# A fused attention and quantised feed-forward kernel: the feed-forward stage written out in full, with three pairs of PSUM banks for gate and up, and with its steps reordered

## The chip, the cores and the metric

The kernel runs on one core of one Trainium2 chip. The metric is the device time of one execution in microseconds (us); the median of three runs of the kernel before is 2051.89 us (2051.29 to 2052.78). A measurement of this kernel tells a difference of about 0.2%, some 4 us, from none.

## What is computed

```python
x = x + xattn(layernorm(x), ctx_2048, Wq, Wk, Wv, Wo)     # 16 x 256 tokens of 512, 16 heads of 128
x = x + ffn(layernorm(x), w_gate, w_up, w_down)

def ffn(x):                                   # w_gate, w_up: 2048 x 512; w_down: 512 x 2048
    gate = q_act(x) @ q_w(w_gate).T
    up   = q_act(x) @ q_w(w_up).T
    inter = silu(gate) * up
    return q_act(inter) @ q_w(w_down).T
# q_act, q_w: block quantisation along the last axis in blocks of 32: a shared power of two from the
# block's largest magnitude, each element rounded to a few bits, clipped (at 7.5 or 6.0), scaled back
```

## The kernel before, in words

The program is written by hand for each of the five queues (TensorE, VectorE, ScalarE, GpSimd and the SyncE queue that issues most DMAs), with semaphores between them. Each queue works strictly in the order written.

**The attention stage** comes first and takes the first 1690 us or so. The change leaves it as it is. At its end every queue goes over into the feed-forward stage.

**The feed-forward stage.** The 4096 tokens are 32 tiles of 128 rows (`TILES`). The 2048 intermediate columns of a tile are four quarters of 512, counted `u = 4 t + k`; two quarters are a pair, `v = 2 t + h`, and there are 64 pairs (`PAIRS`). For a pair the work goes round all engines:

- TensorE: `gate_up` makes one quarter, four matmuls into a gate bank and four into an up bank (line 1097). It may start when the bank pair is free, that is, when VectorE has done `inner` of the quarter two before. For the first quarter of a tile it also waits for the tile's transposed rows (`xqT_loaded`, two buffers).
- ScalarE: `silu` of the gate bank into SBUF (line 688).
- VectorE: `inner` multiplies this with the up bank (line 831). When both quarters of a pair are there, `reduce` takes the magnitudes of the blocks (line 1008), `scales` makes the power (line 876) and its inverse (line 882), and `round_a` rounds one half to fp8 (line 1019).
- GpSimd: `round_b` rounds the other half (line 557).
- VectorE: `clip` of the whole pair to bf16 (line 1028). In the order of VectorE it stands in the next pair, between its two `inner`.
- ScalarE: `scale` copies the powers to bf16 (line 734). GpSimd: `rescale` multiplies the clipped pair with them (line 566); in GpSimd's order `rescale(v-1)` stands ahead of `round_b(v)`.
- SyncE: `transpose_inner` (line 373) transposes the pair by DMA into one of four slots. Behind that of an even pair `2 t` it issues `load_x_tile(t + 2)` (line 356), the transposing DMA of the rows of the tile two further on from a DRAM scratch. Both go by the one queue, in order.
- TensorE: `down` multiplies the pair with the down weights, eight matmuls into one of two banks (line 1220), three pairs behind the gate and up products.
- ScalarE: `move_down` copies the finished sum of a tile to SBUF (line 728). GpSimd: `add_out` adds it to the output in DRAM by an accumulating DMA (line 571).

The last half of the last pair goes another way: TensorE transposes it against an identity matrix (line 1266), and ScalarE and VectorE copy it out. The last two tiles are added to the attention rows, which are still in SBUF, by VectorE (lines 1081, 1085), and stored by plain DMAs (line 393).

The last attention batch is normalised and quantised within the feed-forward stage: `LAST_STEPS` gives after which pair VectorE does a step of it (lines 837 to 871), `POOL_STEPS` after which pair GpSimd does one (lines 480 to 499). So VectorE and GpSimd are written out for the first 18 tiles (`STRAIGHT`) and loop over the rest; TensorE and ScalarE loop from tile 4, SyncE from tile 2.

Of the kernel before, what the change touches and what calls it, by code (L numbers as in the profile page):

```python
# [36 lines left out]
ALU = mybir.AluOpType  # L37
# [21 lines left out]
STRAIGHT = 18  # L59
# [22 lines left out]
def build(nc, kvt, wattn, wffn, xtok, out):  # L82
# [4 lines left out]
    with ctx:  # L87
# [25 lines left out]
        identb = sb("identb", P, BF16)  # L113
# [34 lines left out]
        def free_part(chunk, part, pc, pieces):  # L148
# [5 lines left out]
        iqT = free_part(2, 1, 4, 4).bitcast(BF16)  # L154
        sil = free_part(0, 0, 0, 2).bitcast(F32)
# [5 lines left out]
        i_scale = sb("inner_scale", 32, BF16)[:, :]  # L161
# [8 lines left out]
        pLast = [bS[:, 0:256].bitcast(BF16), bC[:, 0:256].bitcast(BF16)]  # L170
        last_rows = [acc[:, 0:D], acc[:, D:2 * D]]
        gate = [bPT, bQK]
        up = [bX, bV]
# [16 lines left out]
            iqT_loaded0 iqT_loaded1 iqT_loaded2 iqT_loaded3 down_done d_moved out_stored0 out_stored1 last_q last_tr last_moved last_added last_stored0 last_stored1"""  # L190
        sm = {n: sem(n) for n in names.split()}
        sm["first_loaded"] = [sem(f"first_loaded{pc}") for pc in range(PIECES)]
# [71 lines left out]
        def _(eng):  # L264
# [103 lines left out]
            def transpose_inner(v, at):  # L368

                wait_apart(eng, "i_q", v + 1)  # L370
                if not isinstance(v, int) or v >= 4:
                    wait_apart(eng, "down_done", v - 3)
                eng.dma_start_transpose(half(iqT, at, 1024).rearrange("p (j f) -> p j f", j=8),
                                        half(iq, at % 2, 1024)).then_inc(sm[f"iqT_loaded{at}"], 16)

            def tile(t, at, more=True, last=False):
                transpose_inner(2 * t, 2 * at)
                if more:
                    load_x_tile(t + 2, at)
                if not last:  # L380
                    transpose_inner(2 * t + 1, 2 * at + 1)
# [6 lines left out]
            tile(TILES - 2, 0, more=False)  # L388
            tile(TILES - 1, 1, more=False, last=True)
            eng.wait_ge(sm["x1_stored"], 16 * B)  # L390
            for j in range(2):
                eng.wait_ge(sm["last_added"], j + 1)
                eng.dma_start(out[TILES - 2 + j], last_rows[j]).then_inc(sm[f"last_stored{j}"], 16)
            for at in range(2):
                eng.wait_ge(sm[f"out_stored{at}"], 8 * TILES - 16)
            for j in range(2):
                eng.wait_ge(sm[f"last_stored{j}"], 16)
# [3 lines left out]
        def _(eng):  # L401
            eng.memset(ident[:, :], 0.0).then_inc(sm["ident_ready"], 1)
            eng.memset(identb[:, :], 0.0).then_inc(sm["ident_ready"], 1)
            eng.memset(powers[:, 0:1], -0.5).then_inc(sm["ident_ready"], 1)
            eng.memset(powers[:, 1:2], 1e-5).then_inc(sm["ident_ready"], 1)
            eng.wait_ge(sm["ident_ready"], 4)
            for m in (ident, identb):
                eng.affine_select(out=m[:, :], in_=m[:, :], compare_op=ALU.not_equal, fill=1.0, base=0,
                                  pattern=[[-1, P]], channel_multiplier=1).then_inc(sm["ident_ready"], 1)
# [151 lines left out]
            def rescale(v, h):  # L561

                wait_apart(eng, "i_clip", v + 1)
                wait_apart(eng, "i_scale_done", v + 1)
                q = half(iq, h, 1024)
                eng.tensor_tensor(by_block(q), by_block(q), spread(i_scale), ALU.mult).then_inc(sm["i_q"], 1)  # L566
# [7 lines left out]
            def tile(t, at, out_=True, last_batch=False):  # L574
                for h in range(2):
                    v = 2 * t + h
# [3 lines left out]
                    if last_batch and v == 0:  # L580
                        store_x1(B - 1, acc[:, 0:2 * D].rearrange("p (t d) -> p t d", t=2))
                    step = POOL_STEPS.get(v) if last_batch else None
                    if step == "rstd":
                        tile_rstd(B - 1)
                    for j in range(2):
                        if step == f"round{j}":
                            x_round(TILES - 2 + j, j)
                        if step == f"rescale{j}":
                            x_rescale(TILES - 2 + j)
                if out_:  # L590
                    add_out(t - 2, at)

            tile(0, 0, out_=False, last_batch=True)
            tile(1, 1, out_=False, last_batch=True)
            eng.wait_ge(sm["x1_stored"], 16 * B)
            for t in range(2, STRAIGHT):
                tile(t, t % 2, last_batch=True)
            with eng.Fori(STRAIGHT // 2, TILES // 2) as m:
                for a in range(2):
                    tile(2 * m + a, a)  # L600
# [3 lines left out]
            eng.tensor_tensor(by_block(q), by_block(q), spread(i_scale[:, 0:NBLK]), ALU.mult).then_inc(sm["i_q"], 1)  # L604

        @block.scalar
        def _(eng):
# [75 lines left out]
            def silu(t, k):  # L683
                u = 4 * t + k
                eng.wait_ge(sm["gu_done"], u + 1)
                if not isinstance(t, int) or u >= 2:
                    eng.wait_ge(sm["inner_done"], u - 1)
                eng.activation(half(sil, k % 2), gate[k % 2][:, :], ACT.Silu).then_inc(sm["silu_done"], 1)
# [41 lines left out]
            def scale(v):  # L730
                eng.wait_ge(sm["i_pow_done"], v + 1)
                if not isinstance(v, int) or v > 0:
                    eng.wait_ge(sm["i_q"], v)
                eng.activation(i_scale, i_pow, ACT.Copy, scale=16.0).then_inc(sm["i_scale_done"], 1)

            def tile(t, at, begun=0, out_=True):
                for h in range(2):
                    for k in (2 * h, 2 * h + 1):
                        if k >= begun:
                            silu(t, k)  # L740
                    if out_ and h == 0:
                        move_down(t - 2, at)
                    scale(2 * t + h)

            tile(0, 0, begun=2, out_=False)
            tile(1, 1, out_=False)
            tile(2, 0)
            tile(3, 1)
            with eng.Fori(2, TILES // 2) as m:
                for a in range(2):  # L750
                    tile(2 * m + a, a)
            eng.wait_ge(sm["last_tr"], 1)
            eng.activation(half(iqT, 6), pLast[0], ACT.Copy).then_inc(sm["last_moved"], 1)
# [3 lines left out]
        def _(eng):  # L757
            eng.wait_ge(sm["ident_ready"], 6)
# [67 lines left out]
            def inner(t, k):  # L826
# [4 lines left out]
                eng.tensor_tensor(half(inter, k), up[k % 2][:, :], half(sil, k % 2), ALU.mult  # L831
# [190 lines left out]
            def clip(t, at, h):  # L1022
                v = 2 * t + h
                eng.wait_ge(sm["i_round_a"], v + 1)
                wait_apart(eng, "i_round_b", v + 1)
                if not isinstance(t, int) or t >= 1:
                    wait_apart(eng, f"iqT_loaded{2 * (1 - at) + h}", 8 * (t - 1 - (1 - at)) + 16)
                eng.tensor_scalar(half(iq, h, 1024), half(i8, h, 1024), 7.5 / 64, -7.5 / 64, ALU.min, ALU.max  # L1028
                                  ).then_inc(sm["i_clip"], 1)
# [17 lines left out]
            def tile(t, at, begun=0, last_batch=False):  # L1047
                for h in range(2):
                    v = 2 * t + h
                    if 2 * h >= begun:  # L1050
                        inner(t, 2 * h)
                    if h == 1:
                        clip(t, at, 0)
                    elif not (isinstance(t, int) and t == 0):
                        clip(t - 1, 1 - at, 1)
                    if 2 * h >= begun:
                        inner(t, 2 * h + 1)
                    reduce(v, h)
                    scales(v)
                    round_a(v, h)  # L1060
                    if last_batch and v == 0:
                        add_rows(B - 1, 0)
                        add_rows(B - 1, 1)
                    if last_batch and v in LAST_STEPS:
                        last_step(*LAST_STEPS[v])

            tile(0, 0, begun=2, last_batch=True)
            for t in range(1, STRAIGHT):
                tile(t, t % 2, last_batch=True)
            with eng.Fori(STRAIGHT // 2, TILES // 2) as m:  # L1070
                for a in range(2):
                    tile(2 * m + a, a)
# [232 lines left out]
```

## Time and profile before

| what | value |
|---|---|
| median of the runs | 2051.89 us |
| the profiled execution | 2051.55 us |
| its span in the profile | 2050.0 us, so 1.55 us lie around it |
| granted TensorE clock, mean | 0.999 of full speed |
| instructions | 45754 |
| DMA traffic | 193.26 MB, mean 94 GB/s |

Times in the profile count from the span's start. PE is TensorE's matmuls, PEld its weight loads, DVE is VectorE, ACT is ScalarE, POOL is GpSimd, SPq the queue of SyncE. All buffers of the feed-forward stage lie in the space of the attention weights, so the profile names them all attn_weights; which one it is follows from the line. A row of the timeline has the start, the duration, the engine, the line, the operation, what it writes and reads, and in brackets how long the engine was idle before it and what released it. Matmul ends are modelled, so the time of a group of matmuls is best read from the start of one group to the start of the next.

### The profile page before, as it was taken

To read this page: it belongs to the slowest core of one execution; us is meant where nothing else is said; L and a number is where in the kernel's file an instruction comes from. 1 tells how busy PE (TensorE), PEld (TensorE's weight loads), DVE (VectorE), ACT (ScalarE), POOL (GpSimd) and SP (SyncE) were. 2 spreads that over 40 slices of the span, in tenths; PEclk is the share of its full clock that TensorE was granted. 3 is DMA by queue.
4 is the path that set the end of the run, shared out by engine and by line. 5 is a ranking of instruction groups with operands and counts; after the bars stand their busy time and mean duration, and the time that the engine had idled before them with its cause. 6 is when DMAs were issued, how large, how long until landed. Compare 5 with 4: busy or idle time off the path is not lost. (4 is left out here: it accounts for less than half of the span.)

```text
span 2050.0 us, 45754 instructions
## 1 busy us (share of the span) xinstructions
PE 2021.3 (99%) x15430; PEld 1506.2 (73%) x15430; DVE 1536.7 (75%) x3340; ACT 1000.2 (49%) x2682; POOL 740.2 (36%) x881
## 2 busy tenths in 40 slices
PE   8999999999999999999999999999999999999998
PEld 6888878788888888878888888888888874444443
DVE  6767777777777877777777777776665558888887
ACT  8955545455555455555454555455555453222332
POOL 5422232323333333323333333331111006777776
PEclk9999999999999999999999999999999999999999
DMA  8834444444444444444444445443333274454554
GB/s 257 211 72 84 86 91 86 91 90 86 90 91 91 91 88 87 91 91 91 91 86 87 90 89 91 91 86 72 69 70 71 55 168 80 78 92 83 88 87 85
DMA packets 455038, 193.26 MB, mean 94 GB/s; under 512 B 418400, under 2 KB 431200, under 8 KB 454848
## 3 DMA queue, kind: packets, MB, share of 16 engines
q1 hardware_dynamic: 432640, 139.52, 35.3%
q0 software_dynamic: 15872, 44.97, 9.2%
q10 hardware_dynamic: 6336, 6.29, 1.0%
q8 instruction: 112, 1.84, 0.4%
q14 instruction: 78, 0.64, 0.1%
HBM read 61.21 MB, written 27.26 MB: 43 GB/s over the span
## 5 line engine op out<-in xcount | busy, mean ns | idle before, releaser
L1097 PE MATMUL b_qk<-kvT,attn_weights 128*128 128x256 f16 x3072 | 377.2, 273 | 3.5 <-DVE qk L762 2.9
L1097 PE MATMUL b_v<-attn_weights,kvT 128*128 128x256 f16 x3072 | 377.2, 273 | 0.0
L1097 PE MATMUL b_qk<-xT,attn_weights 128*128 128x256 f16 x3072 | 377.2, 273 | 0.0
L654 ACT ACTIVATE prob<-b_s,nmax 128x256 f32<-128x256 f32 x514 | 239.2, 470 | 276.1 <-DVE nmax L923 274.2
L1097 PEld LDWEIGHTS b_qk<-kvT,attn_weights 128*128 128x128 f16 x3072 | 300.2, 98 | 92.7 <-issue 4.9
L950 DVE SCALAR_TENSOR_TENSOR psplit<-prob,rrec,psplit 128x256 f16<-128x256 f32 x514 | 306.5, 637 | 79.2 <-ACT psplit L664 79.2
L762 DVE SCALAR_TENSOR_TENSOR qk<-b_qk,qk 128x512 f16<-128x512 f32 x256 | 176.7, 690 | 246.0 <-ACT qk L610 238.4
L610 ACT ACTIVATE qk<-b_qk 128x512 f16<-128x512 f32 x256 | 152.5, 596 | 426.4 <-PE b_qk L1097 426.2
L1097 PEld LDWEIGHTS b_qk<-xT,attn_weights 128*128 128x128 f16 x3072 | 300.6, 98 | 34.8
L1097 PEld LDWEIGHTS b_v<-attn_weights,kvT 128*128 128x128 f16 x3072 | 300.6, 98 | 34.8
L664 ACT ACTIVATE psplit<-prob,rrec 128x256 f16<-128x256 f32 x514 | 233.0, 500 | 67.8 <-DVE rrec L943 67.8
L1097 PE MATMUL b_c<-probT,vbuf 128*128 128x256 f16 x1554 | 212.0, 273 | 3.1 <-DMA probT<-psplit 3.0
L1097 PE MATMUL b_s<-qk 128*128 128x256 f16 x1542 | 210.3, 273 | 0.0
L1152 PE MATMUL b_o<-attn_weights,cbuf 128*128 128x512 f16 x768 | 186.6, 379 | 0.0
L1152 PE MATMUL b_w<-attn_weights,cbuf 128*128 128x512 f16 x768 | 186.6, 379 | 0.0
L923 DVE TENSOR_REDUCE nmax<-b_s 128x2 f32<-128x512 f32 x257 | 177.1, 689 | 3.7 <-PE b_s L1097 3.3
L1097 PEld LDWEIGHTS b_c<-probT,vbuf 128*128 128x128 f16 x1554 | 151.3, 98 | 23.2 <-DMA probT<-psplit 4.5
L1097 PEld LDWEIGHTS b_s<-qk 128*128 128x128 f16 x1542 | 150.9, 98 | 17.4
L463 POOL TENSOR_TENSOR ffn_magic_rounded<-ffn_y,ffn_magic_rounded 128x512 f32<-128x512 f32 x48 | 60.7, 1265 | 230.1 <-DVE ffn_magic_rounded L823 230.1
L566 POOL TENSOR_TENSOR attn_weights<-attn_weights,inner_scale 128x1024 bf16<-128x1024 bf16 x63 | 120.2, 1908 | 49.2 <-DVE attn_weights L1028 43.1
L421 POOL DMA_DIRECT2D kvrow<-kvt x61 | 35.6, 584 | 241.9 <-DVE kvT L762 218.7
L1152 PEld LDWEIGHTS b_w<-attn_weights,cbuf 128*128 128x128 f16 x768 | 75.1, 98 | 63.8
(133 smaller groups left out, 2642.0 us busy)
## 6 DMA issues: line engine op xcount, KB each, us to landing
ffn_w<-wffn SPq DMA_DIRECT2D x48, 256.0 KB, 2.9
acc<-xtok POOLq DMA_DIRECT2D x16, 512.0 KB, 4.9
out<-acc POOLq DMA_DIRECT2D x16, 512.0 KB, 3.3
xrow<-xtok POOLq DMA_DIRECT2D x31, 256.0 KB, 3.2
kvrow<-kvt POOLq DMA_DIRECT2D x61, 128.0 KB, 2.4
out<-attn_weights POOLq DMA_DIRECT2D x30, 256.0 KB, 4.5
stage<-wattn SPq DMA_DIRECT2D x12, 512.0 KB, 4.6
ffn_scratch<-ffn_t SPq DMA_DIRECT2D x48, 128.0 KB, 2.5
```

What stands on the lines that cost most here:

```text
L421: eng.dma_start(kvrow[:, :], kvt[bass.ds((r + QPB) & (NQ - 1), 1), :, :].rearrange("g p f -> p (g f)")).then_inc(sm["kv_loaded"], 16)
L463: eng.tensor_tensor(wr, wy[:, :], wc, ALU.add).then_inc(sm["ffn_add"], 1)
L566: eng.tensor_tensor(by_block(q), by_block(q), spread(i_scale), ALU.mult).then_inc(sm["i_q"], 1)
L610: eng.activation(dst, src, ACT.Copy, scale=scale).then_inc(sm[done], 1)
L654: last = eng.activation(half(prob, q, 256), half(bS, q, 256), ACT.Exp, bias=nmax[:, q:q + 1], scale=1.0, accum_out=rsum[:, q:q + 1])
L664: eng.activation(p_part(k, q, 0), half(prob, q, 256), ACT.Copy, scale=rrec[:, q:q + 1]).then_inc(sm["p_hi"], 1)
L762: eng.scalar_tensor_tensor(out=dst, in0=src, scalar=scale, in1=hi_part, op0=ALU.mult, op1=ALU.subtract).then_inc(sm[done], 1)
L923: eng.tensor_reduce(nmax[:, :], bS[:, :].rearrange("p (q f) -> p q f", q=2), AX_X, ALU.max, negate=True).then_inc(sm["max_done"], 1)
L950: last = eng.scalar_tensor_tensor(out=p_part(k, z, 1), in0=half(prob, z, 256), scalar=rrec[:, z:z + 1], in1=p_part(k, z, 0), op0=ALU.mult, ...
L1097: last = eng.matmul(out, l, r, start=(a == 0), stop=(a == len(pairs) - 1))
L1152: last = eng.matmul(o_bank[tile_][:, :], l, r, start=(u % 8 == 0 and at == 0), stop=(u % 8 == 7 and at == len(pairs) - 1))
```

## The change

The feed-forward stage is written out for all 64 pairs on all queues. Three pairs of banks serve gate and up (`GU_BUF`, `GU_FREE`), twelve slots the transposed pairs (`INNER_SLOTS`). VectorE does both `inner`, then `reduce`, then the `clip` of the pair before, then `scales` and `round_a`. GpSimd does `round_b(v)` ahead of `rescale(v-1)`. ScalarE does `scale(v-1)` between the two `silu` of pair v, and the scales have two buffers. TensorE does no `down` in pairs 0 to 3, 36, 40, 44 and 48, so that `down` is four pairs behind, later five to eight, and eight are left at the end. The last four tiles are added by VectorE from the banks, and the transposition by TensorE falls away.

```diff
-STRAIGHT = 18
+INNER_SLOTS = 12
+NO_DOWN = (0, 1, 2, 3, 36, 40, 44, 48)
+DOWN_AT = {v: d for d, v in enumerate(v for v in range(PAIRS) if v not in NO_DOWN)}
+MOVE_AT = {v: d // 2 for v, d in DOWN_AT.items() if d % 2}
+BEHIND = range(len(DOWN_AT), PAIRS)
+LAST = TILES - 4
+GU_BUF = [u % 2 if u < 4 else (u - 2) % 3 for u in range(2 * PAIRS)]
+GU_FREE = [max([w + 1 for w in range(u) if GU_BUF[w] == GU_BUF[u]], default=0) for u in range(2 * PAIRS)]
...
-        gate = [bPT, bQK]
-        up = [bX, bV]
+        gate = [bPT, bQK, bS]
+        up = [bX, bV, bC]
...
 # sync
-            tile(0, 0)
-            tile(1, 1)
-            with eng.Fori(1, TILES // 2 - 1) as m:
-                for a in range(2):
-                    tile(2 * m + a, a)
...
+            for v in range(PAIRS):
+                transpose_inner(v)
+                if v % 2 == 0 and v // 2 + 2 < TILES:
+                    load_x_tile(v // 2 + 2, v // 2 % 2)
...
 # gpsimd
-                    if not (isinstance(v, int) and v == 0):
-                        rescale(v - 1, 1 - h)
-                    round_b(v, h)
...
+            def pair(v):
+                round_b(v, v % 2)
+                if v > 0:
+                    rescale(v - 1, (v - 1) % 2)
...
+                if v - 1 in MOVE_AT:
+                    add_out(MOVE_AT[v - 1], MOVE_AT[v - 1] % 2)
...
 # scalar
+            for v in range(PAIRS):
+                for k in range(2 * (v % 2), 2 * (v % 2) + 2):
+                    if v > 0:
+                        silu(v // 2, k)
+                    if v > 0 and k % 2 == 0:
+                        scale(v - 1)
+                if v in MOVE_AT:
+                    move_down(MOVE_AT[v], MOVE_AT[v] % 2)
...
 # vector
+            def pair(v):
+                t, h = v // 2, v % 2
+                if v > 0:
+                    inner(t, 2 * h)
+                    inner(t, 2 * h + 1)
+                reduce(v, h)
+                if v > 0:
+                    clip(v - 1)
+                scales(v)
+                round_a(v, h)
+                if v == 0:
+                    add_rows(B - 1, 0)
+                    add_rows(B - 1, 1)
+                if v in LAST_STEPS:
+                    last_step(*LAST_STEPS[v])
+
+            def add_down(j):
+                eng.wait_ge(sm["down_done"], 2 * (LAST + j) + 2)
+                if j == 0:
+                    eng.wait_ge(sm["x1_stored"], 16 * B)
+                eng.tensor_tensor(last_rows[j], o_bank[j % 2][:, :], last_rows[j], ALU.add).then_inc(sm["last_added"], 1)
...
 # tensor
+            for v in range(PAIRS):
+                for u in range(2 * v, 2 * v + 2):
+                    if u >= 3:
+                        gate_up(u // 4, u % 4, u // 4 % 2)
+                if v in DOWN_AT:
+                    down(DOWN_AT[v])
+            for d in BEHIND:
+                down(d)
```

## Rows read from the trace of the kernel before

**Rows 1.** The page, part 1: busy time, share of the span, instructions.
```profile
PE 2021.3 (99%) x15430; PEld 1506.2 (73%) x15430; DVE 1536.7 (75%) x3340; ACT 1000.2 (49%) x2682; POOL 740.2 (36%) x881
```

**Rows 2.** Waits of PE, 1700 to 2050: us in total, times, longest.
```profile
PE b_pt L1097 <- DVE attn_weights L831: 8.6, 11, 2.0
PE b_w L1220 <- DMA attn_weights<-attn_weights: 3.3, 1, 3.3
```

**Rows 3.** Timeline, one pair of the looped part.
```profile
1985.55 1.89 PE L1220 MATMUL b_w<-attn_weights 128*128 128x512 bf16 x8
...
1988.27 0.67 DVE L831 TENSOR_TENSOR attn_weights<-b_v,attn_weights 128x512 f32<-128x512 f32 x1
...
1988.97 1.22 DVE L1008 TENSOR_REDUCE inner_amax<-attn_weights 128x32 f32<-128x1024 f32 x1
...
1990.22 0.34 DVE L876 TENSOR_SCALAR inner_pow<-inner_amax 128x32 int32<-128x32 int32 x1
...
1990.60 0.18 DVE L882 TENSOR_SCALAR inner_inv<-inner_pow 128x32 int32<-128x32 int32 x1
...
1990.73 1.89 PE L1220 MATMUL b_o<-attn_weights 128*128 128x512 bf16 x8
...
1991.12 1.42 POOL L557 TENSOR_TENSOR attn_weights<-attn_weights,inner_inv 128x512 fp8e4<-128x512 f32 x1 [0.59 <-DVE inner_inv L882]
...
1992.87 0.69 DVE L1028 TENSOR_SCALAR attn_weights<-attn_weights 128x1024 bf16<-128x1024 fp8e4 x1 [0.64 <-POOL attn_weights L557]
```

**Rows 4.** Timeline, end of the stage.
```profile
2040.61 2.33 PE L1220 MATMUL b_w<-attn_weights 128*128 128x512 bf16 x8 [3.32 <-DMA attn_weights<-attn_weights]
...
2046.75 0.69 DVE L1085 TENSOR_TENSOR acc<-b_w,acc 128x512 f32<-128x512 f32 x1 [2.49 <-PE b_w L1220]
```

**Rows 5.** Timeline, start of the stage, quarters 1, 5 and 6, and VectorE's pair 1.
```profile
1695.47 1.03 PE L1097 MATMUL b_v<-attn_weights 128*128 128x512 bf16 x4
...
1696.53 0.60 ACT L688 ACTIVATE attn_weights<-b_qk 128x512 f32<-128x512 f32 x1 [1.34 <-PE b_v L1097]
...
1697.16 0.69 DVE L831 TENSOR_TENSOR attn_weights<-b_v,attn_weights 128x512 f32<-128x512 f32 x1 [1.36 <-ACT attn_weights L688]
...
1704.58 1.22 DVE L1008 TENSOR_REDUCE inner_amax<-attn_weights 128x32 f32<-128x1024 f32 x1
...
1707.73 1.04 PE L1097 MATMUL b_pt<-attn_weights 128*128 128x512 bf16 x4 [1.09 <-DVE attn_weights L831]
```

**Rows 6.** Timeline, the rescaling of pair 2 and the two transposing DMAs behind it.
```profile
1714.20 1.90 POOL L566 TENSOR_TENSOR attn_weights<-attn_weights,inner_scale 128x1024 bf16<-128x1024 bf16 x1 [1.22 <-DVE attn_weights L1028]
...
1716.20 1.23 SPq L373 DMA_TRANSPOSE attn_weights<-attn_weights  x1
...
1717.62 1.19 SPq L356 DMA_TRANSPOSE attn_weights<-x_scratch  x1
```

**Rows 7.** Line 356, issue to landing, of the one at 1717.62.
```profile
DMA to landing us min/median/max: 2.9/2.9/2.9
```

**Rows 8.** Line 356, issue to landing, of the twelve from 1904 to 2018.
```profile
DMA to landing us min/median/max: 3.6/4.1/4.5
```

**Rows 9.** Line 571 (`add_out`), all 30: durations, and issue to landing.
```profile
L571 POOL DMA_DIRECT2D out<-attn_weights x30: 861/1182/1219, 1728.3 to 2039.3; - x30
...
DMA to landing us min/median/max: 3.8/4.5/4.8
```

**Rows 10.** Timeline, VectorE beside GpSimd, pair 16.
```profile
1786.92 1.47 POOL L557 TENSOR_TENSOR attn_weights<-attn_weights,inner_inv 128x512 fp8e4<-128x512 f32 x1 [0.53 <-DVE inner_inv L882]
...
1787.40 1.02 DVE L876 TENSOR_SCALAR x_pow<-x_amax 128x16 int32<-128x16 int32 x1
```

**Rows 11.** Timeline of POOL, then of DVE, in the attention stage.
```profile
535.04 1.05 POOL L470 TENSOR_TENSOR ffn_b<-ffn_magic_rounded,ffn_scale 128x512 bf16<-128x512 f32 x1 [3.26 <-DMA ffn_t<-ffn_b]
536.05 1.23 POOL L497 TENSOR_TENSOR x_quantised<-x_quantised,x_scale 128x512 bf16<-128x512 bf16 x1
...
535.43 2.13 DVE L950 SCALAR_TENSOR_TENSOR psplit<-prob,rrec,psplit 128x256 f16<-128x256 f32 x2 [0.31 <-ACT psplit L664]
```

More of the change, by code:

```diff
@@ L572, in add_out @@
                               accum_op=ALU.add).then_inc(sm[f"out_stored{at}"], 16)
[L574 to L600 removed]
+            def pair(v):
[3 more added lines that the diff above has]
+                if v == 0:
+                    store_x1(B - 1, acc[:, 0:2 * D].rearrange("p (t d) -> p t d", t=2))
+                step = POOL_STEPS.get(v)
+                if step == "rstd":
+                    tile_rstd(B - 1)
+                for j in range(2):
+                    if step == f"round{j}":
+                        x_round(TILES - 2 + j, j)
+                    if step == f"rescale{j}":
+                        x_rescale(TILES - 2 + j)
+                if v == 4:
+                    eng.wait_ge(sm["x1_stored"], 16 * B)
+                if v - 1 in MOVE_AT:
+                    add_out(MOVE_AT[v - 1], MOVE_AT[v - 1] % 2)
+            for v in range(PAIRS):
+                pair(v)
             wait_apart(eng, "i_clip", PAIRS)
@@ L603, in _ @@
             q = half(iq, 2)
-            eng.tensor_tensor(by_block(q), by_block(q), spread(i_scale[:, 0:NBLK]), ALU.mult).then_inc(sm["i_q"], 1)
+            eng.tensor_tensor(by_block(q), by_block(q), spread(i_scale[:, 32:32 + NBLK]), ALU.mult).then_inc(sm["i_q"], 1)
+            for t in range(LAST):
+                if t not in [MOVE_AT.get(v - 1) for v in range(PAIRS)]:
+                    add_out(t, t % 2)
         @block.scalar
@@ L731, in scale @@
                 eng.wait_ge(sm["i_pow_done"], v + 1)
[L732 to L753, printed above, removed]
+                if v >= 2:
+                    eng.wait_ge(sm["i_q"], v - 1)
+                eng.activation(half(i_scale, v % 2, 32), i_pow, ACT.Copy, scale=16.0).then_inc(sm["i_scale_done"], 1)
+            for v in range(PAIRS):
[6 more added lines that the diff above has]
+                    move_down(MOVE_AT[v], MOVE_AT[v] % 2)
+            scale(PAIRS - 1)
+            for t in range(LAST):
+                if 2 * t + 1 in BEHIND:
+                    move_down(t, t % 2)
         @block.vector
         def _(eng):
-            eng.wait_ge(sm["ident_ready"], 6)
+            eng.wait_ge(sm["ident_ready"], 4)
             def lo(dst, src, hi_part, scale, ready, value, done):
@@ L1045, in last_step @@
                     x_clip(t)
[L1047 to L1072, printed above, removed]
-            clip(TILES - 1, 1, 1)
+            def pair(v):
[8 more added lines that the diff above has]
+                round_a(v, h)
+                if v == 0:
+                    add_rows(B - 1, 0)
[5 more added lines that the diff above has]
+                if j == 0:
+                    eng.wait_ge(sm["x1_stored"], 16 * B)
+                eng.tensor_tensor(last_rows[j], o_bank[j % 2][:, :], last_rows[j], ALU.add).then_inc(sm["last_added"], 1)
+            for v in range(PAIRS):
+                pair(v)
+            add_down(0)
+            clip(PAIRS - 1)
             wait_apart(eng, "i_clip", PAIRS)
```

140 lines of the change are left out of this document (55 added, 85 removed).

## The prediction

> **What bounds the kernel now.** The page comes first: TensorE is busy for 99% of the span [rows 1], so time can only come from its gaps. The waits of TensorE from 1700 on tell where they are. 8.6 us in 11 waits go to VectorE's `inner`, which frees the two bank pairs, and 3.3 us in one wait to the last transposed pair but one [rows 2]. The timeline tells how near the other engines are. In the looped part one pair takes 5.18 us from `down` to `down` [rows 3], which is 24 matmuls, or three groups of eight at 1.73 us. In the same pair VectorE and GpSimd close a circle of nearly this length: `inner` at 1988.27, `reduce`, pow, inv, GpSimd's `round_b`, and `clip` from 1992.87 to 1993.56, with the next `inner` beside its end, so some 5.2 us [rows 3]. So TensorE bounds the looped part with no room, and each extra step for the last batch in pairs 4 to 33 opens a gap.
>
> **What TensorE could give.** Gaps before: 1.1 us at quarter 6 [rows 5], the rest of the 8.6, and the end. There TensorE stands 3.3 us ahead of the `down` at 2040.61 [rows 4] and then waits for the transposition and the copies. With eight `down` left, 8 x 1.73 = 13.8 us, the last pair's round is covered. From the end of the last quarter it needs 3.8 us to the inverse (below), 1.76 + 1.9 for GpSimd's two steps, 1 to 2 for `clip` and the half rescaling and some 3.2 for the DMA, about 12.5. The last addition stays as it is: from 2046.75 to the span's end at 2050.0 are 3.25 us [rows 4], and 0.2 us from TensorE to VectorE. `down` left out of pairs 36, 40, 44 and 48 only moves 4 x 1.73 = 6.9 us to the end, and is a gain if the quarters really run ahead by that. The loops written out I cost at nothing: the looped pairs ran at 5.18, TensorE's own pace.
>
> **VectorE and GpSimd.** In the new order GpSimd need not wait for `clip`. From the end of the inverse (1990.78) `round_b` ends at 1992.54, so 1.76 us [rows 3], and `rescale` takes 1.90 more [rows 6]. Then `clip`, pow and inv (0.6 + 0.2 + 0.2) close a round of 4.65 us. That is 0.5 under TensorE, so lateness is made good at 0.5 a pair, and three bank pairs bear about 3 us of it. The banks thus no longer bind: that wait goes.
>
> **What is late next.** `load_x_tile` stands in SyncE's queue behind `transpose_inner` of an even pair, and that behind `rescale`. Before, `rescale(v-1)` came ahead of `round_b(v)`; now it comes after it, and `clip(v-1)` after `reduce(v)`. The circle goes over odd pairs v = 2T+1 and ends at the first quarter of tile T+2. From the end of the last quarter of v:
> - to `silu` 0.20 and on to `inner` 0.63 (1695.47 + 0.86, 1696.53, 1697.16) [rows 5];
> - `inner` to `reduce` 0.70, reduce 1.2, `clip` 0.69, pow and inv 0.2 each when GpSimd is idle [rows 3]: together 3.8;
> - `round_b` and `rescale` 3.65;
> - `rescale` ended at 1716.10; the pair's transposition went out at 1716.20, the load at 1717.62, and it landed 2.9 later [rows 6, 7]: 4.4, and 0.1 to TensorE.
>
> The sum is 11.95 us. TensorE arrives there after one `down` and two more pairs, 1.73 + 10.36 = 12.1 us. The room is 0.15 to 0.2 us in every four pairs. Before, `rescale(v-1)` waited neither for pair v's inverse nor for its `round_b`, and TensorE shows no wait for this load [rows 2].
>
> The landing is the widest term. Twelve loads in the looped part took 3.6 to 4.5 us, median 4.1 [rows 8], against 2.9 [rows 7]. Those twelve went out together with an `add_out`, which lands 4.5 us after its issue [rows 9]. Now `add_out` follows `rescale` of an odd pair, and a load that of an even pair, a pair (5.2 us) later and 1.5 us further on, so it is over. I take 2.9. The pattern shifts after pair 36: at pairs 39 and 47 the two fall together, 1.3 us each.
>
> **The steps for the last batch.** They now cost what they push an odd pair back. From inverse to the step are 0.76 us, and about 0.8 us is free. `stats`, `aggr` and `reduce` (0.7 or less) fit. The others run against GpSimd. The row shows x_pow, 0.17 us of work, taking 1.02 and ending at 1788.42, just behind `round_b` (1788.39) [rows 10]. And who waits takes turns: VectorE's two instructions of line 950 took 2.13, the first ended behind line 470, GpSimd's 497 was stretched to 1.23, and the second came behind it [rows 11]. The Trainium skill, page "SBUF — State Buffer", section "Who interferes with whom", has an exclusive lock held for the whole instruction between GpSimd and a VectorE `tensor_scalar` in a two-port mode. By that rule, the trace agrees (1.02 for 0.17); its advice to let whoever is off the critical path block is not met by this change, in which `rescale` now stands directly behind `round_b`.
> So x_scales (pairs 16 and 27) gets its pow in behind `round_b`, and then its inv waits for the whole `rescale`: 2.3 us late at pair 17, and 2.3 at pair 28 of which 1.7 are left at 29. Bounds: 0.7 if all three small instructions get in together, 2.3 if not; I take 2.3 by the turns in the row. `apply` (12, 20) is 0.65 late, `clip` (22) 0.45, GpSimd's rounding and rescaling (18, 24) 0.5; those at 29, 31 and 33 fall on even pairs and are made good. The room of 0.2 taken off for each turn, and TensorE passing the delay of one tile on to the next, the delays leave D = 0.45 + 2.1 + 0.45 + 0.3 + 1.5 = 4.8 us by tile 16. After that the odd tiles win back 0.2 in each of 7 turns and lose 2 x 1.3 + 0.4 in two of them: D = 6.4. The four pairs without `down` lie in even tiles, and so do nothing for the odd ones: their 6.9 us is idle time.
>
> **Start.** VectorE's reduce of pair 1 is at 1704.58 [rows 5]. With 1.2 for it, `clip`, pow and inv the inverse is there at 1706.9, `round_b` ends at 1708.6, `rescale(0)` at 1710.5, and the load of tile 2 has landed 4.5 later: its first quarter starts at 1715.0, that of tile 3 at 1715.0 + 10.36 = 1725.4. I count from there.
>
> **Sum.** Tile 31 starts at 1725.4 + 28 x 10.36 + 6.4 = 2021.9. Then 14 groups (four quarters, two `down`, eight more): 24.2, to 2046.1, and 3.45 to the end: span 2049.5, run 2051.1 against 2051.55 of the profiled execution, whose time is 0.3 under the median. So 2051 on the median's scale: no change that can be measured. All that is gained at the end and on the banks is spent on the load.
>
> **Rivals.**
> - The load lands in time and TensorE runs through. For it: the room is positive by my sum, and 0.3 us less in a circle of 12 is enough. Each 0.1 us of room is worth some 1.3 us in the end. With room 0.5 the delays before tile 16 shrink to about 3 and 2 us are won back after: 2047. With a full 1.0 and small steps all 6.9 us of moved `down` count: 1725.4 + 290.1 - 6.9 + 27.6 = 2036.2, run 2038. Middle 2043. Chance 0.36.
> - Slower: the load takes 4.1 us as in the looped part [rows 8], because the pair's own transposition just ahead or another DMA is in its way. Then the circle is 8.64 + 13.2 = 21.8 us in four pairs instead of 20.7, tile 31 starts at 1725.4 + 14 x 21.8 = 2030.6 plus 5 us of late steps, and the run takes 2065. It decides from 0.35 us more than my 11.95 on (2056). Chance 0.26.
> - The forecast, the two within 0.2% of each other (2047.8 to 2056): 0.38.
> - That the change doesn't do what it says, for instance that VectorE's round and not TensorE's bounds all pairs: its round of 4.65 speaks against it, and it lies within the bounds above.
>
> A measurement of this kernel tells about 0.2% (4 us) from none. The range that leaves out 2 in 10 goes from 2040 to 2061; of it the forecast's own is 2047 to 2056. The bounds of x_scales (2.7 us in sum) and of the landing (1.2 us a turn, 16 us) are in it.
>
> **What would show each step.** TensorE's waits: hardly any on line 831; instead waits of 0.5 to 2 us on the landing of x_scratch at first quarters of tiles, and none of 3.3 us at the end. SyncE: line 356 (in its new place) issued 1.4 us behind line 373, landing in 2.5 to 3 us, and over 4 at pairs 39 and 47. VectorE: x_inv lasting near 2 us at pairs 16 and 27. Pairs of 5.18 us where no wait stands, 3.45 without `down`. I am wrong if TensorE waits for no load (then it is faster, about 2038 to 2043), or if the load takes 4 us throughout.

## The result, and the profile after

The change made the kernel slower: 2061.89 us (2059.92 to 2064.11, 4 runs) against 2052.18 (2051.29 to 2052.78, 4 runs), a ratio of 1.0051, interval [1.0039, 1.0062]. The forecast was 2051, its range 2040 to 2061, missed by 0.9. The profiled execution took 2059.92, its span is 2058.3.

From one execution to another the last stage begins at another time (tile 0's first matmul between 1691.75 and 1696.10 us in all these profiles). So beside the medians I use the **stage**, the span of the profiled execution less that start: 2050.0 - 1692.22 = 357.8 us before, 2058.3 - 1691.82 = 366.5 after.

The page of the changed kernel, against [rows 1]:

```profile
PE 2024.4 (98%) x15422; PEld 1509.3 (73%) x15422; DVE 1523.2 (74%) x3341; ACT 999.8 (49%) x2679; POOL 739.5 (36%) x877
...
q8 instruction: 122, 2.00, 0.4%
```

It moves too little to tell anything. TensorE's waits from 1690 on do, against [rows 2] (us in total, times, longest):

```profile
PE b_pt L1083 <- DMA attn_weights<-x_scratch: 8.2, 5, 4.5
PE b_s L1083 <- DMA attn_weights<-x_scratch: 6.1, 3, 3.2
PE b_qk L1083 <- DMA attn_weights<-x_scratch: 3.9, 3, 2.9
PE b_w L1209 <- DMA attn_weights<-attn_weights: 1.1, 1, 1.1
```

Not one wait on `inner` is left; 18.2 us in 11 waits stand in front of first quarters, on `load_x_tile`. The bank waits went, as the change means them to, and of the waits at the end (5.0 us in three before) 1.1 is left. Waits on one kind of transfer took their place.

What such a wait leaves behind is in the next view, TensorE's timeline at tile 2:

```profile
1714.16 1.89 PE L1083 MATMUL b_pt<-attn_weights 128*128 128x512 bf16 x4 [4.46 <-DMA attn_weights<-x_scratch]
1715.84 1.91 PE L1083 MATMUL b_x<-attn_weights 128*128 128x512 bf16 x4
1717.55 1.91 PE L1083 MATMUL b_qk<-attn_weights 128*128 128x512 bf16 x4
1719.26 1.11 PE L1083 MATMUL b_v<-attn_weights 128*128 128x512 bf16 x4
...
1721.93 1.03 PE L1083 MATMUL b_s<-attn_weights 128*128 128x512 bf16 x4
```

Four matmuls start 1.71 us after the four before them instead of 0.86. The windows say why (busy us of PE, PEld, DVE, ACT and POOL, then the granted clock, DMA share, GB/s); the first begins within this wait and the second is behind it, the third is behind one of 2.90, the fourth behind one of 2.20, the last behind one of 3.19:

```profile
1713.00:1716.00 3.00, 1.84 (x5) 0.73 (x6) 2.82 (x5) 0.00 (x0) 1.87 (x2) 0.50 0.25 55
1716.00:1719.40 3.40, 3.40 (x10) 1.20 (x8) 0.76 (x2) 0.71 (x2) 2.84 (x2) 0.50 0.30 57
...
1920.30:1924.60 4.30, 4.30 (x13) 1.61 (x12) 0.69 (x1) 0.71 (x2) 2.66 (x2) 0.60 0.28 53
...
1942.30:1945.50 3.20, 2.99 (x14) 1.39 (x15) 1.90 (x5) 0.72 (x2) 2.85 (x3) 1.00 0.63 74
...
1965.00:1968.60 3.60, 3.60 (x10) 1.31 (x9) 0.33 (x1) 0.35 (x1) 3.09 (x2) 0.53 0.37 72
```

A granted clock of 0.50 is 1.2 instead of 2.4 GHz. It is there behind three of the waits, and not behind the one of 2.20. At half clock half of the time is lost: tile 3 starts 12.95 us after tile 2 instead of 10.36, so 2.6 us, and some 1.7 us in each of the other two stretches. That is 6.0 us which no view of waits shows.

### The profile page after: what moved, and what is told of

Its sections match the earlier page's. It is cut to its first block, busy times and chain, and to the rows that moved or that the text cites. A ratio compares the mean times of both kernels' runs of the same rounds, so it can differ in the third digit from the quotient of the medians.

```text
span 2058.3 us, 44906 instructions
## 1 busy us (share of the span) xinstructions
PE 2024.4 (98%) x15422; PEld 1509.3 (73%) x15422; DVE 1523.2 (74%) x3341; ACT 999.8 (49%) x2679; POOL 739.5 (36%) x877
## 4 chain that ended last, share of the span: by engine, by line
PE 86%; DMA 4%; issue 3%; DVE 2%; POOL 2%; ACT 2%; SPq 1%; DVEq 0%; POOLq 0%; ACTq 0%
PE b_qk L1083 32%; PE b_v L1083 17%; PE b_c L1083 9%; PE b_s L1083 9%; PE b_w L1138 8%; PE b_o L1138 8%; POOL attn_weights L565 2%; DMA attn_weights<-attn_weights 1%; DMA attn_weights<-x_scratch 1%; PE b_o L1209 1%; PE b_pt L1083 1%; PE b_x L1083 1%; PE b_w L1209 1%; DMA probT<-psplit 1%; SPq L383 0%
## 5 line engine op out<-in xcount | busy, mean ns | idle before, releaser
L556 POOL TENSOR_TENSOR attn_weights<-attn_weights,inner_inv 128x512 fp8e4<-128x512 f32 x64 | 92.7, 1448 | 92.4 <-DVE inner_inv L874 90.5
L1138 PEld LDWEIGHTS b_o<-attn_weights,cbuf 128*128 128x128 f16 x768 | 75.1, 98 | 63.8 <-DVE cbuf L753 0.5
```

The costliest lines, as they stand in the source:

```text
L556: eng.tensor_tensor(by_block(half(i8, 2 * h + 1)), by_block(half(inter, 2 * h + 1)), spread(i_inv[:, NBLK:2 * NBLK]), ALU.mult, saturate=False
L1138: last = eng.matmul(o_bank[tile_][:, :], l, r, start=(u % 8 == 0 and at == 0), stop=(u % 8 == 7 and at == len(pairs) - 1))
```

## Experiments

All are built on the changed kernel. Spans are of the profiled execution; "before" was run beside each batch (medians 2051.34, 2051.86 and 2050.74).

**1. The load first.** On SyncE, `load_x_tile` is put ahead of `transpose_inner`, so that it no longer stands behind `rescale`.

```diff
             for v in range(PAIRS):
-                transpose_inner(v)
                 if v % 2 == 0 and v // 2 + 2 < TILES:
                     load_x_tile(v // 2 + 2, v // 2 % 2)
+                transpose_inner(v)
```

> The changed kernel with one swap in SyncE's order: the load of a tile's rows stands ahead of the transposition of the even pair, no longer behind it, so it goes out one pair (5.2 us) earlier. Theory 'load circle' (the load behind the rescaling holds TensorE): the 18 us of waits for x_scratch vanish, with them the stretches at half clock; three banks bear the late steps of up to 2.3 us, and the four pairs without a down product become a gain. Span near 2036 to 2039, time 2038 to 2041. Rival 'round' (the new order of VectorE and GpSimd, with rescale directly behind round_b and the port held, bounds the pairs): other waits, on line 823 or on the transposed pairs, take the place of those removed, and the time stays at 2055 or more.

Measured: 2036.91 us (2036.55 to 2040.21), ratio to before 0.9929 [0.9912, 0.9945]; span 2038.6, stage 343.4, 23 us less than the changed kernel's. These are all of TensorE's waits from 1690 on:

```profile
PE b_w L1209 <- DMA attn_weights<-attn_weights: 1.5, 1, 1.5
PE b_s L1083 <- DVE attn_weights L823: 1.2, 1, 1.2
PE b_qk L1083 <- DVE attn_weights L823: 1.0, 2, 0.8
```

The loads themselves land no sooner, 2.6 to 6.2 us after their issue and mostly near 4, and 21 of the 30 now go out 1.6 to 2.0 us behind an `add_out`. But they go out 4.2 to 7.8 us ahead of the quarter that needs them, and TensorE waits for none. The load circle is the cause, and with it out of the way the change is worth 0.7%. The rival, that VectorE's round bounds the pairs, falls: only three short waits on line 823 are left, 2.2 us in all.

**2. TensorE kept busy in the longest waits.** 16, 9 and 10 dummy matmuls ahead of the waits of tiles 2, 21 and 25, into banks that are written afresh behind them.

```diff
-                if k == 0:
-                    eng.wait_ge(sm[f"xqT_loaded{at}"], 8 * (t - at) + 16)
                 if GU_FREE[u] > 0:
                     eng.wait_ge(sm["inner_done"], GU_FREE[u])
+                if k == 0:
+                    for a in range({2: 16, 21: 9, 25: 10}.get(t, 0)):
+                        eng.matmul(gate[GU_BUF[u]][:, :], fw[:, 0:P], ffn_rhs(0, 0), start=True, stop=True)
+                    eng.wait_ge(sm[f"xqT_loaded{at}"], 8 * (t - at) + 16)
```

> The changed kernel with matmuls whose result is overwritten, put into three waits for the load (16 before tile 2, 9 before tile 21, 10 before tile 25: 3.5, 1.9 and 2.2 us), all shorter than the wait they stand in. The output is the same. Theory 'clock' (waits of 2.9 us and more are followed by a stretch at half clock, 6.8 and 3.4 us long, which costs 2.6 + 1.7 + 1.7 us): the granted clock stays at 1.0 and the kernel is 5 to 6 us faster than the changed kernel, at 2054 in the profile, 2056 in the median. Rival (the half clock costs nothing, since the load circle goes over VectorE and the DMA and TensorE would only wait longer): no difference from 2060 to 2062, with longer waits for x_scratch behind it.

Measured: 2054.88 us (2052.23 to 2057.6, 10 runs), ratio 1.0018 [1.0009, 1.0028], so 7.0 us less than the changed kernel by work that computes nothing; span 2053.4, stage 359.1. The window behind the first wait, against the two of 0.50 above:

```profile
1716.00:1719.40 3.40, 2.74 (x13) 1.29 (x14) 2.59 (x6) 0.71 (x2) 2.27 (x2) 1.00 0.39 75
```

The half clock is gone, and with it the 6 us read from the windows: from tile 2 to 3, 21 to 22 and 25 to 26 TensorE takes 2.58, 1.69 and 1.69 us less than in the changed kernel. The other 1.4 us of the stage are not the clock's; 1.2 are won at tile 19, whose load landed in 2.6 us here and in 3.9 there, for which run 9 gives a reason.

**3. No products left out.** NO_DOWN is (0, 1, 2, 3), four pairs are left for the end, and VectorE adds two tiles.

```diff
-NO_DOWN = (0, 1, 2, 3, 36, 40, 44, 48)
+NO_DOWN = (0, 1, 2, 3)
...
-LAST = TILES - 4
+LAST = TILES - 2
...
```

The lines left out make the four last additions and stores two.

> The changed kernel without the four pairs 36, 40, 44 and 48 that leave out a down product: down stays four pairs behind, four are left at the end, and VectorE adds the last two tiles instead of four. Theory 'load circle': the down products left out bought only idle time. Tile 31 starts 6 us earlier relative to tile 3 (3.4 of half clock, 2.6 of two loads that no longer meet add_out), less the 6.9 that TensorE now works instead of idling, which cost nothing; at the end four down products (6.9 us) no longer cover the last pair's round of 12.5, so TensorE waits some 5 us there. In sum 2052 to 2055, 7 us faster than the changed kernel. Rival (the four pairs are a gain in the changed kernel as written): slower than it, by up to 6.9 us, 2066 or more.

Measured: 2057.74 us (2055.54 to 2058.88, 6 runs), ratio 1.0029 [1.0016, 1.0041]; span 2057.2, stage 365.1. Faster than the changed kernel by 4 us in the medians and 1.4 in the stage, less than I had expected. Tile 31 starts at 2023.20 instead of 2029.45, though four products more are done by then: in the changed kernel they were indeed idle time. What I had wrong is the end, for which I had counted one wait of 5 us:

```profile
PE b_w L1209 <- DMA attn_weights<-attn_weights: 5.0, 1, 5.0
PE b_o L1209 <- DMA attn_weights<-attn_weights: 3.4, 1, 3.4
...
2038.82 3.60 PE L1209 MATMUL b_o<-attn_weights 128*128 128x512 bf16 x8 [3.38 <-DMA attn_weights<-attn_weights]
```

There are two waits, and the eight matmuls behind each take 3.6 us instead of 1.89, at half clock. From tile 31 on it takes 34.0 us instead of 28.9. So the eight products do cover the last pair's round but for the 1.1 us above, and are worth 5.1 us there.

**4. Two additions put off.** The `add_out` of pairs 39 and 47 go out one pair later, away from a load.

```diff
-                if v - 1 in MOVE_AT:
-                    add_out(MOVE_AT[v - 1], MOVE_AT[v - 1] % 2)
+                late = {40: 38, 48: 46}.get(v)
+                if late is not None:
+                    add_out(MOVE_AT[late], MOVE_AT[late] % 2)
+                elif v - 1 in MOVE_AT and v not in (39, 47):
+                    add_out(MOVE_AT[v - 1], MOVE_AT[v - 1] % 2)
```

> The changed kernel with the two accumulating DMAs that fall into an odd pair (39 and 47) put off by one pair. Theory 'load meets add_out': the loads of tiles 21 and 25 land in 2.7 us instead of 4.5 and 4.8; the waits before tiles 21 and 25 shrink from 2.9 and 3.2 to 1.1 to 1.4, so no stretch at half clock follows, and the time falls by 1.8 + 2.0 + 3.4 = 6 to 7 us, to 2053 in the profile. Rival (they land late for another cause, such as the pair's own transposition): no difference.

Measured: 2053.61 us (2051.8 to 2054.86, 10 runs), ratio 1.0009 [1.0, 1.0019]; span 2051.9, stage 359.9, so 8 us by the medians and 6.6 by the stage for two DMAs moved by 5 us. The changed kernel's timeline at pair 39 shows what they did there:

```profile
1913.27 1.41 POOL L571 DMA_DIRECT2D out<-attn_weights  x1
1913.48 1.24 SPq L383 DMA_TRANSPOSE attn_weights<-attn_weights  x1
...
1914.90 1.19 SPq L364 DMA_TRANSPOSE attn_weights<-x_scratch  x1
...
1919.45 1.04 PE L1083 MATMUL b_qk<-attn_weights 128*128 128x512 bf16 x4 [2.90 <-DMA attn_weights<-x_scratch]
```

The addition, the transposition and the load go out within 1.6 us, the load lands 4.5 us later, TensorE waits 2.90 and then works at half clock. In this run the same load lands in 2.8 us, that of pair 47 in 2.7 instead of 4.8. The waits of tiles 21 and 25 are 1.7 and 2.1 us shorter, and 3.4 us of half clock behind them are gone. That is 7.2, more than the 6.6 of the stage, since two other things moved. Behind the wait of tile 2 half clock lasted for less of the work (1.1 us won), and behind a wait of 2.07 us at tile 23 there is half clock here (1.7 us lost), where the changed kernel had none behind its 2.20. Run 9 has the same: half clock behind 2.22 us at tile 23, none behind 2.38 at tile 21. First this run at tile 23, then run 9 at tile 21:

```profile
1938.14 1.04 PE L1086 MATMUL b_pt<-attn_weights 128*128 128x512 bf16 x4 [2.07 <-DMA attn_weights<-x_scratch]
...
1939.30:1942.60 3.30, 3.30 (x9) 1.14 (x8) 1.11 (x2) 0.71 (x2) 3.19 (x2) 0.50 1.06 159
...
1920.72 1.04 PE L1085 MATMUL b_qk<-attn_weights 128*128 128x512 bf16 x4 [2.38 <-DMA attn_weights<-x_scratch]
...
1920.70:1924.60 3.90, 3.88 (x18) 1.78 (x19) 2.03 (x5) 0.93 (x3) 2.94 (x2) 1.00 0.67 71
```

So between 2.07 and 2.38 us the length of a wait doesn't tell what it costs.

**5. Two bank pairs,** on top of run 1.

```diff
-GU_BUF = [u % 2 if u < 4 else (u - 2) % 3 for u in range(2 * PAIRS)]
+GU_BUF = [u % 2 for u in range(2 * PAIRS)]
```

> Built on the changed kernel with load_x_tile ahead of transpose_inner (span 2038.6 us), but with two gate and up bank pairs in turn instead of three. Theory: the third pair of banks is worth something only where VectorE is late by a step for the last batch, up to 2.3 us in an odd pair; with two pairs TensorE waits on line 823 again. By hand over the pairs with steps: 5 to 6 us, so a span of 2044 (2041 to 2047), and some ten waits of TensorE on VectorE's inner between 1700 and 2000. Rival: the later rescaling alone (a VectorE round of 4.65 us against TensorE's 5.18) had removed the bank waits, and the third pair is worth nothing: 2038 to 2040.

Measured: 2043.24 us (2041.29 to 2045.78), ratio 0.9956 [0.994, 0.9973]; span 2044.2, stage 351.6.

```profile
PE b_pt L1083 <- DVE attn_weights L823: 7.5, 9, 1.9
PE b_w L1209 <- DMA attn_weights<-attn_weights: 2.1, 1, 2.1
```

The third pair of banks is worth 6 us by the medians and 8 by the stage, about as expected.

**6. No products left out,** the edit of run 3 on top of run 1.

> Built on the changed kernel with load_x_tile ahead of transpose_inner, but no down product is left out of pairs 36, 40, 44 and 48: four stay behind at the end, and VectorE adds the last two tiles only. Theory: now that TensorE is the bound in the looped part, the moved products pay in full: the quarters run 6.9 us ahead and the products cover the last pair's round. Without them the end waits as it did where this was undone behind the slow load (3.4 + 5.0 us in two waits on transposed pairs, and half clock behind them), so a span of 2038.6 + 8.4 - 1.5 + 1 to 2 = 2047 (2045 to 2049). Rival: the end's cover is worth nothing since the last pair's round is short: 2038 to 2041.

Measured: 2050.02 us (2048.53 to 2052.35, 10 runs), ratio 0.9994 [0.9984, 1.0003]; span 2048.2, stage 355.8. By that, with the load first, the moved products are worth 12.5 us of the stage: tile 31 starts 321.4 us after tile 0 instead of 314.1, and the end is 5.2 longer. (0.9 of it is not theirs: between tiles 0 and 1 TensorE waits for a transposition of the attention stage in this execution.) What a product left out brings with the load late and in time shows in one pair of rows each. Tile 18, which has no product in its first pair, in the changed kernel:

```profile
1886.83 1.04 PE L1083 MATMUL b_qk<-attn_weights 128*128 128x512 bf16 x4 [0.46 <-DMA attn_weights<-x_scratch]
...
1897.39 1.04 PE L1083 MATMUL b_s<-attn_weights 128*128 128x512 bf16 x4 [1.76 <-DMA attn_weights<-x_scratch]
```

and in run 1, with the load first and the same products left out:

```profile
1881.19 1.03 PE L1083 MATMUL b_qk<-attn_weights 128*128 128x512 bf16 x4
...
1889.82 1.03 PE L1083 MATMUL b_s<-attn_weights 128*128 128x512 bf16 x4
```

From first quarter to first quarter 10.56 us there, 8.63 here.

**7 and 8. The old order of clip and rescale,** once with the load first (7), once with the load where the change has it (8). Three bank pairs and the moved products stay. VectorE and GpSimd are changed together; neither was tried alone.

```diff
@@ VectorE
                     inner(t, 2 * h)
+                    clip(v - 1)
                     inner(t, 2 * h + 1)
                 reduce(v, h)
-                if v > 0:
-                    clip(v - 1)
@@ GpSimd
-                round_b(v, v % 2)
                 if v > 0:
                     rescale(v - 1, (v - 1) % 2)
+                round_b(v, v % 2)
```

> Built on the changed kernel with load_x_tile ahead of transpose_inner, but with the old order on both engines: clip between the two inner, and rescale ahead of round_b. Three bank pairs and the moved products stay. Theory: VectorE's and GpSimd's circle is then 5.2 us again, as long as TensorE's pair, so late steps are not made good; three bank pairs bear some 3 us of them, the rest shows as waits on line 823: a span of 2044 (2041 to 2047). Rival: the later rescaling is worth nothing once the load is out of its way: 2038 to 2040.

> Built on the changed kernel as it is (load_x_tile behind transpose_inner), with the old order on both engines: clip between the two inner, and rescale ahead of round_b. Theory: it is the later rescaling that makes the load late, by the 1.76 us of round_b and the clip behind reduce; undone, TensorE waits for no load from tile 3 on but for VectorE's inner, as in the run before this one: a span of 2044 to 2048, 10 to 14 us under the changed kernel. Rival: the load is late by the order on SyncE alone, whatever GpSimd does: 2055 or more.

Measured: run 7, 2053.98 us (2051.42 to 2056.62, 10 runs), ratio 1.0011 [1.0001, 1.002]; run 8, 2054.0 (2052.7 to 2055.27, 10 runs), ratio 1.0011 [1.0002, 1.0021]. The waits of run 8:

```profile
PE b_s L1082 <- DVE attn_weights L823: 5.7, 8, 1.7
PE b_qk L1082 <- DVE attn_weights L823: 4.7, 4, 1.4
PE b_pt L1082 <- DVE attn_weights L823: 3.4, 4, 1.4
PE b_w L1208 <- DMA attn_weights<-attn_weights: 2.3, 1, 2.3
```

The mechanism holds: with the old order no load is waited for in run 8, though SyncE's order is the slow one, so it is the later clip and rescaling that make the load late. The size was wrong in both: expected were spans of 2044, and of 2044 to 2048, measured 2055.0 and 2052.5. I had counted only late steps against the old circle of 5.2 us [rows 3] and let the moved products pay in full; but a pair without its product is 3.45 us of TensorE, and VectorE's circle is longer than that. Quarters of pairs 36 and 37 in run 8:

```profile
1888.87 1.04 PE L1082 MATMUL b_s<-attn_weights 128*128 128x512 bf16 x4 [0.16 <-DVE attn_weights L823]
...
1891.09 1.04 PE L1082 MATMUL b_pt<-attn_weights 128*128 128x512 bf16 x4 [0.32 <-DVE attn_weights L823]
...
1894.37 1.04 PE L1082 MATMUL b_qk<-attn_weights 128*128 128x512 bf16 x4 [1.39 <-DVE attn_weights L823]
```

The 1.73 us that the product left free come back as 0.16 + 0.32 + 1.39 of waits. The four runs make a table (median, and stage in us):

| | load behind the transposition | load first |
|---|---|---|
| old order of clip and rescale | 2054.0, 358.5 | 2054.0, 358.9 |
| later rescaling | 2061.9, 366.5 | 2036.9, 343.4 |

Moving the load alone is worth nothing; rescaling later alone costs 8; both together win 17. And against the kernel before, at 2051.9 beside these runs, everything but the later rescaling (run 8) wins nothing either.

**9. The code moved.** Of the 30 landings of `load_x_tile` in the changed kernel 19 are 2.6 to 3.0 us, and eleven 3.1 to 4.8. Two of these are the ones of run 4; beside each of the other nine (3.1 to 4.0) a packet of an instruction queue (q8 or q14) starts between 0.5 us before and 2.3 us after the load's issue. Two more loads had one there and landed in 2.7 and 3.0. In runs 3 and 4 too, every load over 3.0 us has such a packet. Since the code is written out, q8 has such a packet about every 28 us, twelve from 1700 on; in the kernel before it had two, at 1724.6 and 1792.1. To see whether the packets or the work of those pairs did it, TensorE's code was pushed on by 80 instructions.

```diff
         def _(eng):
+            for a in range(80):
+                eng.wait_ge(sm["ident_ready"], 1)
             eng.wait_ge(sm["ident_ready"], 4)
```

> The changed kernel with nothing altered but 80 waits that are already satisfied, put at the very beginning of TensorE's program, while it waits for GpSimd's first memsets anyway. The code behind them lies 80 instructions further on, so the packets of the instruction queue q8, which come every 28 us, shift. In the run with dummy products 32 instructions more moved them from 1725.0 to 1721.8 us, so 80 should put them near 1717, 1745, 1773, 1802, 1829, 1859, 1885, 1917, 1947, 1980 and 2008. Theory: a load_x_tile that lands in over 3.0 us is one with an instruction packet beside it; the loads at 1809, 1893, 1924 and 2015 (4.0, 3.9, 3.6, 3.5 us) then land in 2.6 to 2.9, and that near 1744.5 (2.9) or others beside the new places take 3.3 or more. Those beside packets of q14 (1734, 1883, 1938) stay slow. Time 2058 to 2063. Rival: the slow landings come from the order of the other work at those pairs: the same loads stay slow.

Measured: 2060.28 us (2059.53 to 2061.08), ratio 1.0044 [1.0027, 1.0061]; span 2058.9, stage 364.3. Against the tiles the packets of q8 moved by some 5.5 us, not 8, so the places that I had named for them were missed, and the load near 1744.5 stayed fast (2.7). But the four loads that were named became fast: 2.6, 2.6, 2.7 and 2.6 us, and the three beside packets of q14 stayed slow (3.5, 3.7, 3.8). The DMA view of the changed kernel from 1809 to 1813 (packets, MB, share; then the landing):

```profile
q8 instruction: 1, 0.02, 1.5%
...
attn_weights<-x_scratch SPq DMA_TRANSPOSE x1, 4.0
```

and of this run from 1812 to 1816, the same load, where only the queue of the transfers has packets:

```profile
q1 hardware_dynamic: 1460, 0.36, 44.5%
...
attn_weights<-x_scratch SPq DMA_TRANSPOSE x1, 2.6
```

The other way round, the load of tile 27, 2.6 us in the changed kernel, is slow in this run (1985 to 1989):

```profile
q8 instruction: 1, 0.02, 1.5%
...
attn_weights<-x_scratch SPq DMA_TRANSPOSE x1, 3.8
```

The slow landings follow the instruction packets, not the pairs. The time hardly changes: some loads are faster, others slower.

**10. A ninth product left out,** in pair 52, on top of run 1.

```diff
-NO_DOWN = (0, 1, 2, 3, 36, 40, 44, 48)
+NO_DOWN = (0, 1, 2, 3, 36, 40, 44, 48, 52)
```

> Built on the changed kernel with load_x_tile ahead of transpose_inner (span 2038.6 us, 1.5 us of it a wait of the down products on the last transposed pair): the down product is left out of pair 52 as well, so nine pairs stay behind at the end. Theory: TensorE bounds the pairs, so the ninth product moves for nothing and fills the last wait: 1.5 us less, a span of 2037 (2036.5 to 2038). Rival: a pair without its product is bound by VectorE's round and the wait only moves: 2038.6.

Measured: 2036.16 us (2035.23 to 2037.47), ratio 0.9929 [0.9912, 0.9945]; span 2033.6, stage 341.9, 1.5 less than run 1, and the wait at the end is gone; one load landed 7.1 us after its issue, and TensorE waited 0.4 us for it. The 5 us between the two spans are mostly the start of the stage, which came 3.5 us earlier in this execution. By their medians runs 1 and 10 can't be told apart; both beat both kernels.

## Why the prediction was wrong

The circle that the forecast names was right. The step that failed is the price of its waits: idle time of TensorE counted at its length, where the half clock behind it costs 6.0 us more, the most of the 8.8 us by which the span was missed. Smaller misses stand beside it. Point by point, by its own steps:

- **"The banks thus no longer bind: that wait goes."** Right; run 5 prices the third pair at 6 us.
- **"The room is 0.15 to 0.2 us in every four pairs."** Right. Runs 1 and 8 cut the circle at two places, and the waits on x_scratch vanish in both. In the changed kernel the load of tile 29 went out at 2004.80, landed 2.9 us later and was needed at 2008.01, so it had 0.2 to 0.3 us to spare, and tiles follow one another there at TensorE's own 10.36.
- **Idle time priced at its length.** The forecast never says so, but every term of its sum does it. Waits of 2.90, 3.19 and 4.46 us cost 1.7, 1.7 and 2.6 us more in half clock, 6.0 in all; run 2 won these 6.0 us by filling the waits. The hint stood in [rows 4]: the `down` behind the wait of 3.32 took 2.33 us where others take 1.89 [rows 3], and the window behind it, in the kernel before, has a granted clock of 0.71:

```profile
2040.50:2044.00 3.50, 3.18 (x16) 1.65 (x16) 1.47 (x3) 0.60 (x1) 1.24 (x1) 0.71 0.79 150
```

  I had read that row for its wait only. The Trainium skill, page "TensorE: Matmul & The Clock Gate", section "HAM oscillation — how this bites in real kernels", describes the pattern: a wait for a DMA can be long enough for the clock to fall, so that the work behind it starts cold. The windows above agree, with 0.50 behind a wait of 4.46.
- **"The loops written out I cost at nothing."** Wrong by its consequence for the DMAs. The code now comes in through the same DMA engines every 28 us, and a load beside such a packet landed in up to 4.0 us instead of 2.7 (run 9). With 0.2 us of room that is a wait. What it costs in all was not measured by itself.
- **"the odd tiles win back 0.2 in each of 7 turns."** Wrong in thought. Room in the circle makes the load land before TensorE comes; TensorE itself, at its own 20.72 us for two tiles, can win nothing back outside the pairs without a product. From tile 17 on the six waits on loads are 0.46, 1.76, 2.90, 2.20, 3.19 and 0.54 us.
- **"At pairs 39 and 47 the two fall together, 1.3 us each."** The place was exact; the landings were 4.5 and 4.8 instead of 2.9, so 1.6 and 1.9, and with the half clock behind them they cost 7.2 us (run 4), where 2.6 was forecast.
- **"its inv waits for the whole `rescale`."** Right, at pairs 16 and 27: near 2 us was forecast, 1.82 and 1.83 came. Pair 16:

```profile
1788.63 1.90 POOL L565 TENSOR_TENSOR attn_weights<-attn_weights,inner_scale 128x1024 bf16<-128x1024 bf16 x1
1788.73 1.82 DVE L874 TENSOR_SCALAR x_inv<-x_pow 128x16 int32<-128x16 int32 x1
```

- **"their 6.9 us is idle time."** Right (run 3, and tile 18 above), and run 6 shows what they bring where the load is in time.
- **Start and end.** Tile 2 was forecast at 1715.0 and started at 1714.16. The end kept one wait that I had taken as covered. From the end of the last quarter to the landing of the last transposition it took 15.1 us and not 12.5: the transposition goes out at 2048.22, 0.3 us behind an `add_out`, and lands in 4.9 us, for which I had 3.2, and the `clip` ahead of it waited 1.3 us for an earlier transposition.

```profile
2047.93 0.86 POOL L571 DMA_DIRECT2D out<-attn_weights  x1
...
2050.17 1.89 PE L1209 MATMUL b_w<-attn_weights 128*128 128x512 bf16 x8
2053.21 1.90 PE L1209 MATMUL b_w<-attn_weights 128*128 128x512 bf16 x8 [1.15 <-DMA attn_weights<-attn_weights]
```

The account from the forecast span of 2049.5 to 2058.3: start of tile 3, 1.7 (2.6 of clock less 0.9); half clock behind tiles 21 and 25, 3.4; other delays between tiles 3 and 31, 12.2 - 6.4 - 3.4 = 2.4; the last wait 1.15. Sum 8.65, of 8.8. The 2.4 are a difference of two misses: up to tile 17 the delays were 3.7 us where 4.8 was forecast, and behind it 5.2 (without the clock) where 1.6 was. Of these 3.6, 0.9 are the longer landings at pairs 39 and 47 and 1.4 the turns that won nothing back; the rest was not taken apart, and the late loads of tiles 19 and 23 lie in it. The account is that of the profiled execution, the fastest of its four; the median lies 2.0 us above it, and what these are is open.

Of the rivals, "the load lands in time" didn't happen. It had 2038 for full room, and run 1, where the load is in time, gives 2036.9. The slower rival (2065) was near the result by another way: not by a landing of 4.1 us throughout, but by few late ones and what they leave behind. That it came near is luck.

## What to carry to other kernels

Where a transfer stands in a queue behind work that the change makes later, sum the circle that it closes; if its room is smaller than the spread of its landing, move the transfer before anything else. Price a wait of TensorE not by its length: read the granted clock in the stretch behind each long wait in the kernel at hand; waits of one size can differ in it. And of two parts that are worth nothing or less alone (here the later rescaling and the earlier load), the pair can be worth the most; judge work moved off a pair only by the engine that is next there.

## What the runs showed of the hardware

- Behind waits of TensorE of 2.90 and 3.19 us the granted clock was 0.50 for 3.4 us; by the one of 4.46 us it fell within the wait and stayed at 0.50 for 5.2 us of the work behind it. Behind waits of 2.07 (run 4) and 2.22 us (run 9) it fell too, behind 2.20 (changed kernel) and 2.38 us (run 9) it stayed at 1.00. Dummy matmuls in the three longest waits kept it at 1.00 and saved 6.0 us of a stage of 366.
- In the changed kernel a transposing DMA of one tile from DRAM landed in 2.6 to 3.0 us, in 4.5 and 4.8 beside an accumulating DMA to the output issued 1.6 us before it (4.1 and 4.5 in run 9), and in 2.7 to 4.0, mostly over 3.1, with an instruction packet near it. With TensorE's code straight such a packet (0.02 MB) came about every 28 us in this stage.
